# Cross attention of a decoder as one written-out row of 32 rounds: another order of its pieces, queries' weights handled apart, the output one round later

## The chip, the cores and the metric

One core of one Trainium2 chip runs the whole program in one launch. The metric is the device time of that core in microseconds (us), the median of several runs. TensorE (PE) multiplies, VectorE (DVE), ScalarE (ACT) and GpSimd (POOL) work on what it leaves, and SyncE (SP) issues the transfers.

## What is computed

Two decoder layers on x of 4 x 512 x 512, six steps with a layer normalisation after each. The change is in the fifth step alone, the cross attention of layer 1:

```python
q = (hidden_states @ Wq).reshape(B, Sq, H, D)            # B 4, Sq 512, H 16, D 128
k = (encoder_hidden_states @ Wk).reshape(B, Skv, H, D)   # Skv 512, inner size 256
v = (encoder_hidden_states @ Wv).reshape(B, Skv, H, D)
q = rmsnorm(q, gq)
k = rmsnorm(k, gk)
scores = jnp.einsum('bqhd,bkhd->bhqk', q, k) * scale
attn = jax.nn.softmax(scores, axis=-1)
out = jnp.einsum('bhqk,bkhd->bqhd', attn, v)
return out.reshape(B, Sq, H * D) @ Wo
# afterwards: x = _layernorm(x + this)
```

## The kernel before

The function `cross_attention` is one of five stages, each a block with its own instruction stream for each engine. It works in 32 rounds: 4 sequences times 8 pairs of heads. A round has two halves that belong to different pairs. The half called x projects pair n+1 (queries, keys and values, means of squares, transposes); the half called y takes pair n through scores, exponentials, values, sums, quotients and the output projection. `body(b, x, y)` writes both for each engine, and `turns` runs it in two nested loops on the chip (`Fori`), with the first and the last half round outside. Between sequences `start` transposes the next x, and `finish` normalises the last one on VectorE.

Every product of two float32 numbers is made of three passes of split numbers (`split3`, lines 198 to 200), except probabilities times values and the sums of probabilities, which are plain float32. The high half of a weight comes from ScalarE (`Copy`), the low half from GpSimd (`lo`). One load, one high half and one low half cover queries', keys' and values' weights together (`load_proj`, L1870, L1793).

Waits go by semaphores. The eight banks of PSUM are shared out in a fixed turn: the class `Banks` makes a matrix product wait until the one before it in the same bank has been read (`wait_empty`). Before the change the banks 0 to 2 serve the projections and transposes (`pa`), 3 to 5 the scores, the sums and the output (`pb`), 6 and 7 the values. The sum of the probabilities of a head lies over all rows of a bank, and VectorE takes its quotient there (L1926, `reciprocal`), which frees the bank.

TensorE's order in a round is: scores of both heads, values of head 0, half of the queries, sum 0, values of head 1, sum 1, the other half of the queries, four tiles of keys and values, one tile of output, transposes of keys and then of queries, three tiles of output. VectorE's order is: quotient 0, quotient 1, mean of the queries' squares, low halves of the output, queries' normalisation, one output tile, low halves of the transposes, mean of the keys' squares, three output tiles.

Of the kernel before, what the change touches and what calls it, by code (L numbers as in the profile page):

```python
# [1633 lines left out]
def cross_attention(c):  # L1634
# [8 lines left out]
    nc, d = c.nc, c.d  # L1643
    HP = 2
    G = 16 // HP
    NW = HP * DX
    with ExitStack() as ctx:
        def sb(nm, shape, dt=F32):
            return ctx.enter_context(nc.sbuf_tensor(f"s5_{nm}", shape, dt))

# [21 lines left out]
        sq = sb("squares", [P, T, NW])  # L1672
# [4 lines left out]
        probsT = sb("probsT", [P, HP, T, S])  # L1677
        psum2 = sb("probs_pair_sums", [P, 2, S])
        psum1 = sb("probs_sum", [P, HP, S])
# [4 lines left out]
        consts = c.sem("s5_gains_loaded")  # L1684
        bound_ready = c.sem("s5_bound_ready")
        rawx_in = Count(c.sem("s5_w_proj_loaded"), 48)
        rawo_in = Count(c.sem("s5_w_out_loaded"), 16)
        wx_hi = Count(c.sem("s5_w_proj_hi_ready"), 1)
        wx_lo = Count(c.sem("s5_w_proj_lo_ready"), 1)
        wo_hi = Count(c.sem("s5_w_out_hi_ready"), 1)  # L1690
        wo_lo = Count(c.sem("s5_w_out_lo_ready"), 1)
        ctx_in = Count(c.sem("s5_ctx_loaded"), 16)
        ctx_hi = Count(c.sem("s5_ctx_hi_ready"), 1)
        ctx_lo = c.s5_ctx_lo
        squared = {"q": Count(c.sem("s5_q_squared"), 1), "k": Count(c.sem("s5_k_squared"), 1)}
        ms_ready = {"q": Count(c.sem("s5_q_mean_sq_ready"), 1), "k": Count(c.sem("s5_k_mean_sq_ready"), 1)}
        rs_ready = {"q": Count(c.sem("s5_q_rstd_ready"), 1), "k": Count(c.sem("s5_k_rstd_ready"), 1)}
        q_normed = Count(c.sem("s5_q_normed"), 1)
        f_hi = {"qT": Count(c.sem("s5_qT_hi_ready"), HP), "kT": Count(c.sem("s5_kT_hi_ready"), HP)}
        p_sum = Count(c.sem("s5_probs_summed"), HP)  # L1700
        inv_ready = Count(c.sem("s5_inv_sums_ready"), HP)
        o_hi = Count(c.sem("s5_out_hi_ready"), HP)


        pa, pb = c.ps.part(), c.ps.part()
        pa_keys = [("q", 0), ("q", 1)] + [("kv", t) for t in range(T)] + [("kT", 0), ("kT", 1), ("qT", 0), ("qT", 1)]
        pa.open([(k, i % 3, 1) for i, k in enumerate(pa_keys)], outer=c.x_uses([0, 1, 2]))
        pb_keys = [("e", h, k) for h in range(HP) for k in range(T)] + [("y", t) for t in range(T)]
        uses = [(k, 3 + i % 3, 1) for i, k in enumerate(pb_keys)]
        pb.open(uses[:8] + [(("o", 0), 6, 1), (("o", 1), 7, 1), (("sum", 0), 3, 1), (("sum", 1), 4, 1)] + uses[8:])  # L1710
        block = ctx.enter_context(nc.Block())

        def flat(ap):
            return ap.rearrange("p a n -> p (a n)")

        def side(buf, turn):

            return flat(buf[:, bass.ds(turn % 2, 1), :])

        def load_proj(sp, g):  # L1720
            sp.dma_start(raw_x[:, OQ:OKV].rearrange("p (k n) -> p k n", k=KD),
                         d["l1x_wq"].rearrange("(k p) n -> p k n", p=P)[:, :, bass.ds(g * NW, NW)]).then_inc(rawx_in.sem, 16)
            kv = raw_x[:, OKV:].rearrange("p (k a n) -> p k a n", k=KC, a=2)
            for a, nm in ((0, "l1x_wk"), (1, "l1x_wv")):
                sp.dma_start(kv[:, :, a, :],
                             d[nm].rearrange("(k p) n -> p k n", p=P)[:, :, bass.ds(g * NW, NW)]).then_inc(rawx_in.sem, 16)

        def load_out(sp, g):
            sp.dma_start(raw_o[:, :].rearrange("p (h n) -> p h n", h=HP),
                         d["l1x_wo"].rearrange("(h p) n -> p h n", p=P)[:, bass.ds(g * HP, HP), :]).then_inc(rawo_in.sem, 16)  # L1730

        def turns(eng, start, body, finish):

            start(0)
            body(0, (0, 0), None)
            with eng.Fori(0, B - 1) as b:
                with eng.Fori(0, G - 1) as g:
                    body(b, (b, b * G + (g + 1)), b * G + g)
                start(b + 1)
                body(b, (b + 1, b * G + G), b * G + (G - 1))  # L1740
                finish(b)
            b = B - 1
            with eng.Fori(0, G - 1) as g:
                body(b, (b, g + (b * G + 1)), g + b * G)
            body(b, None, b * G + (G - 1))
            finish(b)

        @block.sync
        def _(sp):
            sp.dma_start(gains[:, 0, :], d["l1x_gq"].broadcast_to([P, DX])).then_inc(consts, 16)  # L1750
# [3 lines left out]
            load_proj(sp, 0)  # L1754
            load_out(sp, 0)

            def next_proj(turn, g):
# [140 lines left out]
        def _(dve):  # L1898
# [8 lines left out]
            def body(b, x, y):  # L1907
# [41 lines left out]
                if x is not None:  # L1949
                    mean_squares(0, "q")  # L1950
# [717 lines left out]
```

## Time and profile before

| | |
|---|---|
| median of 3 runs | 2633.09 us (2633.03 to 2633.87) |
| the profiled execution | 2633.11 us, span 2631.3 us |
| TensorE busy over the span | 2218.0 us (84%) |
| VectorE, ScalarE, GpSimd busy | 1409.2 us (54%), 1211.2 us (46%), 910.4 us (35%) |
| mean granted clock of TensorE | 0.939 of full speed |

The span runs from the first to the last instruction. A share of busy time is a mean over five stages; the cross attention has the stretch from 1193.8 to 2327.9 us.

### The profile page before, as it was taken

To read this page: it belongs to the slowest core of one execution; us is meant where nothing else is said; L and a number is where in the kernel's file an instruction comes from. 1 tells how busy PE (TensorE), PEld (TensorE's weight loads), DVE (VectorE), ACT (ScalarE), POOL (GpSimd) and SP (SyncE) were. 2 spreads that over 40 slices of the span, in tenths; PEclk is the share of its full clock that TensorE was granted. 3 is DMA by queue.
4 is the path that set the end of the run, shared out by engine and by line. 5 is a ranking of instruction groups with operands and counts; after the bars stand their busy time and mean duration, and the time that the engine had idled before them with its cause. 6 is when DMAs were issued, how large, how long until landed. Compare 5 with 4: busy or idle time off the path is not lost. (4 is left out here: it accounts for less than half of the span.)

```text
span 2631.3 us, 35761 instructions
## 1 busy us (share of the span) xinstructions
PE 2218.0 (84%) x12440; PEld 1555.7 (59%) x12440; DVE 1409.2 (54%) x2138; ACT 1211.2 (46%) x2272; POOL 910.4 (35%) x570
## 2 busy tenths in 40 slices
PE   6988989858867878875999999999999999957672
PEld 4564655447756645544777777777777677634241
DVE  4666666545544543542555665556555655543445
ACT  3645455343335643524555545554555555522322
POOL 3524244310013211203555545555555555510101
PEclk9999999979888999987999999999999999978795
DMA  3000000010010000003111111121111111020001
GB/s 107 2 1 1 0 2 1 1 60 1 1 44 4 1 1 1 1 1 114 48 48 43 53 48 48 48 72 48 48 48 48 48 48 48 32 95 1 0 0 64
DMA packets 62365, 84.12 MB, mean 32 GB/s; under 512 B 6132, under 2 KB 41332, under 8 KB 61752
## 3 DMA queue, kind: packets, MB, share of 16 engines
q1 hardware_dynamic: 62264, 82.76, 9.3%
q8 instruction: 65, 1.06, 0.2%
q14 instruction: 36, 0.29, 0.0%
HBM read 74.36 MB, written 4.19 MB: 30 GB/s over the span
## 5 line engine op out<-in xcount | busy, mean ns | idle before, releaser
L1926 DVE RECIPROCAL s_inv_sums<-banks 128x512 f32<-128x512 f32 x64 | 214.8, 3356 | 343.3 <-PE banks L2039 340.0
L1800 POOL TENSOR_TENSOR s_qk_rstd<-s_mean_sq,minus_half 128x8 f32<-128x8 f32 x64 | 118.5, 1851 | 502.1 <-DVE s_mean_sq L1913 502.1
L2032 PE MATMUL banks<-s_probsT,s_v 128*128 128x512 f32 x512 | 231.3, 594 | 0.0
L1863 ACT ACTIVATE s_probsT<-banks,s_minus_bound,s_qk_rstd 128x512 f32<-128x512 f32 x256 | 177.0, 781 | 92.6 <-PE banks L200 88.6
L594 DVE TENSOR_REDUCE s_neg_max<-banks 128x1 f32<-128x512 f32 x256 | 165.4, 684 | 88.1 <-PE banks L660 86.5
L543 ACT ACTIVATE s_probsT<-banks 128x512 f32<-128x512 f32 x256 | 148.7, 600 | 81.6 <-PE banks L674 79.2
L198 PE MATMUL banks<-s_w_proj_hi,xT_hi 128*128 (+1 forms) x512 | 170.8, 334 | 2.9 <-DVE s_ctxT_lo L1974 2.9
L1834 ACT ACTIVATE s_squares<-banks 128x512 f32<-128x512 f32 x64 | 38.3, 598 | 286.1 <-PE banks L200 286.0
L2032 PEld LDWEIGHTS banks<-s_probsT,s_v 128*128 128x128 f32 x512 | 97.6, 191 | 111.1 <-issue 108.5
L1793 POOL TENSOR_TENSOR s_w_proj_lo<-s_w_proj_raw,s_w_proj_hi 128x2048 f32 (+1 forms) x33 | 151.9, 4604 | 14.0 <-ACT s_w_proj_hi L1826 14.0
L1809 POOL TENSOR_TENSOR s_probs_pair_sums<-s_probsT 128x1024 f32<-128x1024 f32 x64 | 151.2, 2362 | 7.2 <-issue 7.2
L199 PE MATMUL banks<-s_w_proj_lo,xT_hi 128*128 (+1 forms) x512 | 145.7, 285 | 0.0
L200 PE MATMUL banks<-s_w_proj_hi,xT_lo 128*128 (+1 forms) x512 | 145.7, 285 | 0.0
L482 POOL TENSOR_TENSOR x_cur<-s_probsT 128x512 f32<-128x512 f32 x64 | 82.0, 1281 | 156.8 <-PE banks L692 110.1
L660 PE MATMUL banks<-s_kT,s_qT 128*128 128x512 f32 x256 | 117.8, 464 | 6.9 <-DVE s_neg_max L594 3.3
L198 PE MATMUL banks<-s_wqkv_hi,xT_hi 128*128 128x512 f32 (+1 forms) x256 | 92.1, 360 | 34.6 <-POOL s_wqkv_lo L464 8.8
L674 PE MATMUL banks<-s_qT,s_kT 128*128 128x512 f32 x256 | 106.3, 415 | 16.4 <-ACT s_qT L536 14.2
L198 PEld LDWEIGHTS banks<-s_w_proj_hi,xT_hi 128*128 128x128 f32 x512 | 98.9, 193 | 18.1 <-issue 18.1
L198 PE MATMUL banks<-s_w_out_hi,s_outT_hi 128*128 (+1 forms) x256 | 104.2, 407 | 5.8 <-DVE s_outT_lo L1933 5.8
L199 PEld LDWEIGHTS banks<-s_w_proj_lo,xT_hi 128*128 128x128 f32 x512 | 99.1, 194 | 14.8 <-issue 14.8
L198 PE MATMUL banks<-s_w_proj_hi,s_ctxT_hi 128*128 (+1 forms) x256 | 101.3, 396 | 7.1 <-ACT s_v L1849 7.1
L1959 DVE TENSOR_TENSOR x_all<-banks,x_all 128x512 f32 (+1 forms) x128 | 85.5, 688 | 35.6 <-PE banks L200 32.3
(412 smaller groups left out, 5938.8 us busy)
## 6 DMA issues: line engine op xcount, KB each, us to landing
s_w_proj_raw<-l1x_wq SPq DMA_DIRECT2D x33, 512.0 KB, 4.6
s_w_out_raw<-l1x_wo SPq DMA_DIRECT2D x33, 512.0 KB, 3.6
s_w_proj_raw<-l1x_wk SPq DMA_DIRECT2D x33, 256.0 KB, 4.8
s_w_proj_raw<-l1x_wv SPq DMA_DIRECT2D x33, 256.0 KB, 5.1
x_all<-x SPq DMA_DIRECT2D x4, 1024.0 KB, 12.7
s_ctxT<-ctxT SPq DMA_DIRECT2D x8, 512.0 KB, 5.6
x_cur<-x_all SPq DMA_DIRECT2D x4, 1024.0 KB, 8.2
out<-x_all SPq DMA_DIRECT2D x4, 1024.0 KB, 4.3
```

What stands on the lines that cost most here:

```text
L198: pe.matmul(out, lhs[0], rhs[0], start=start, stop=False)
L199: pe.matmul(out, lhs[0], rhs[1], start=False, stop=False)
L200: return pe.matmul(out, lhs[1], rhs[0], start=False, stop=stop)
L543: act.activation(probsT[:, h % NPB, k, :], ps.ap(s), ACT.Exp).then_inc(ps.freed(s), 1)
L594: dve.tensor_reduce(nmax[:, h % 2, t, 0:1], ps.ap(s), AX.X, ALU.max, negate=True) \
L660: pe.matmul(ps.ap(s), qT[:, h % NQB, t * P:(t + 1) * P], kT[:, h % NKV, :], start=True, stop=True).then_inc(ps.filled(s), 1)
L1793: pool.tensor_tensor(out, raw, hi.bitcast(F32), ALU.subtract).then_inc(done.sem, 1)
L1800: pool.tensor_tensor(rs[:, j, :, :], ms[:, j, :, :], c.mhalf[:, 0:T * HP].rearrange("p (t h) -> p t h", h=HP), ALU.pow) \
L1809: pool.tensor_tensor(psum2[:, :, :], probsT[:, h, 0:2, :], probsT[:, h, 2:4, :], ALU.add)
L1863: act.activation(probsT[:, h, k, :], pb.ap(("e", h, k)), ACT.Exp, bias=bound[:, 0:1], scale=rs[:, 1, k, h:h + 1]).then_inc(pb.freed(("e", ...
L1926: dve.reciprocal(inv[:, h, :], pb.ap(("sum", h))).then_inc(pb.freed(("sum", h)), 1)
L2032: mm = pe.matmul(pb.ap(("o", h)), v[:, k, h * DX:(h + 1) * DX], probsT[:, h, k, :], start=(k == 0), stop=(k == T - 1))
```

## The change

`cross_attention` alone is written anew. There are no loops on the chip any more: a Python list `seq` holds all pieces of all rounds in one row, and each engine's stream is that row with the pieces that concern it. What else differs:

- The order in a round is another, for all engines at once. The output projection of pair j is done in round j+1, its first tile between the two sums. The first sum stands behind the second half of the queries. The two transposes of the queries (`TQ`) stand between the second and the third tile of keys and values, those of the keys (`TK`) near the end.
- On VectorE the mean of the queries' squares (`MQ`) comes first, then quotient 0 (`R`), an output tile, the queries' normalisation (`NQ`), and quotient 1.
- Banks 0 to 2 now serve x transposes, queries, keys and values, transposes and also the sums, in turn. Scores and output share banks 3 to 5.
- Queries' weights have a load, a high half and a low half of their own (`WQ`), keys' and values' weights others (`WK`).
- x is transposed from `x_all` itself, and not from a copy loaded again. `x_cur` holds squares and sums of probabilities instead.
- GpSimd adds the four tiles of probabilities with three additions of 512 columns, before with one of 1024 and one of 512.
- The layer normalisation after a sequence (`L`) is applied by ScalarE, before by VectorE. Its statistics are taken with each output tile.
- At the stage's start the big loads are issued ahead of the four small ones of the gains.

The values were plain float32 before and are so after.

```diff
-    nc, d = c.nc, c.d
...
+    nc, d, ps = c.nc, c.d, c.ps
...
-        sq = sb("squares", [P, T, NW])
+        sq = c.xcur[:, 0:2, :].rearrange("p a (b n) -> p (a b) n", n=NW)
+        psum = c.xcur[:, 2:2 + HP, :]
...
+        seq = [("X", 0, k) for k in range(KD)] + [("WQ", 0), ("Cx", 0), ("WK", 0)]
+        for j in range(-1, N + 1):
+            now, nxt, prv, border = 0 <= j < N, j + 1 < N, 0 <= j - 1, (j + 2) % G == 0 and j + 2 < N
+            if now:
+                seq += [("E", j, 0, k) for k in range(T)] + [("U", j, 0)]
+            if nxt:
+                seq.append(("Q", j + 1, 0))
+            if now:
+                for k in range(T):
+                    seq.append(("E", j, 1, k))
+                    if prv and k < HP:
+                        seq.append(("OH", j - 1, k))
+                seq += [("U", j, 1), ("V", j, 0)]
+            elif prv:
+                seq += [("OH", j - 1, h) for h in range(HP)]
+            if nxt:
+                seq += [("Q", j + 1, 1), ("MQ", j + 1)]
+            if now:
+                seq += [("SU", j, 0), ("R", j, 0)]
+            if border:
+                seq += [("X", (j + 2) // G, k) for k in range(KD)]
+            if j + 2 < N:
+                seq.append(("WQ", j + 2))
+            if prv:
+                seq.append(("O", j - 1, 0))
+            if nxt:
+                seq.append(("NQ", j + 1))
+            if now:
+                seq += [("SU", j, 1), ("V", j, 1), ("R", j, 1)]
+            if nxt:
+                seq += [("KV", j + 1, 0), ("KV", j + 1, 1), ("TQ", j + 1, 0), ("TQ", j + 1, 1),
+                        ("KV", j + 1, 2), ("KV", j + 1, 3), ("MK", j + 1)]
+            if prv:
+                seq += [("O", j - 1, 1), ("O", j - 1, 2)]
+            if nxt:
+                seq += [("TK", j + 1, 0), ("TK", j + 1, 1)]
+            if prv:
+                seq.append(("O", j - 1, 3))
+            if border:
+                seq.append(("Cx", (j + 2) // G))
+            if j + 2 < N:
+                seq.append(("WK", j + 2))
+            if now:
+                seq.append(("WO", j))
+            if prv and j % G == 0:
+                seq.append(("L", j // G - 1))
+
+        uses, na, nb = [], 0, 0
+        for s in seq:
+            if s[0] in ("X", "Q", "KV", "TK", "TQ", "SU"):
...
+            elif s[0] in ("E", "O"):
+                uses.append((s, 3 + nb % 3, 1))
+                nb += 1
+            elif s[0] == "V":
+                uses.append((s, 6 + s[2], 1))
+        ps.open(uses)
...
+            load_q(0)
+            load_ctx(0)
+            load_kv(0)
             sp.dma_start(gains[:, 0, :], d["l1x_gq"].broadcast_to([P, DX])).then_inc(consts, 16)
             sp.dma_start(gains[:, 1, :], d["l1x_gk"].broadcast_to([P, DX])).then_inc(consts, 16)
             sp.dma_start(gcols[:, 0:1], d["l1x_gq_col"]).then_inc(consts, 16)
             sp.dma_start(gcols[:, 1:2], d["l1x_gk_col"]).then_inc(consts, 16)
...
+            load_out(0)
+            for ph, j, *s in seq:
+                if ph == "WQ" and j + 1 < N:
+                    sp.wait_ge(*wq_lo.after(j, 1))
+                    load_q(j + 1)
+                elif ph == "WK" and j + 1 < N:
+                    sp.wait_ge(*wk_lo.after(j, 1))
+                    load_kv(j + 1)
...
+                        .then_inc(wo_lo.sem, 1)
+                elif ph == "MQ":
+                    rstd(0, "q", j)
...
+                elif ph == "U":
+                    h = s[0]
+                    pool.wait_ge(*ps.released(0, ("E", j, h, T - 1)))
...
+                    pool.tensor_tensor(psum[:, h, :], probs[:, h, 0, :], probs[:, h, 1, :], ALU.add)
+                    pool.drain()
+                    pool.tensor_tensor(psum[:, h, :], psum[:, h, :], probs[:, h, 2, :], ALU.add)
+                    pool.drain()
+                    pool.tensor_tensor(psum[:, h, :], psum[:, h, :], probs[:, h, 3, :], ALU.add).then_inc(p_sum.sem, 1)
+                    pool.drain()
...
+            for ph, j, *s in seq:
+                if ph == "X":
+                    k = s[0]
+                    dve.wait_ge(*x_hi.after(j, k + 1))
+                    dve.tensor_tensor(c.xlo[:, k, :], ps.ap(("X", j, k)), c.xhi[:, k, :].bitcast(F32), ALU.subtract) \
...
+                elif ph == "MQ":
+                    mean_squares(0, "q", j)
...
+                elif ph == "NQ":
...
+                elif ph == "R":
+                    h = s[0]
+                    dve.wait_ge(*ps.full(0, ("SU", j, h)))
+                    if j > 0:
+                        dve.wait_ge(*o_lo.after(j - 1, h + 1))
+                    dve.reciprocal(inv[:, h, :], ps.ap(("SU", j, h))).then_inc(ps.freed(("SU", j, h)), 1)
+                    dve.wait_ge(*ps.released(0, ("SU", j, h)))
+                    dve.wait_ge(*ps.full(0, ("V", j, h)))
+                    dve.tensor_tensor(inv[:, h, :], ps.ap(("V", j, h)), inv[:, h, :], ALU.mult) \
+                       .then_inc(ps.freed(("V", j, h)), 1)
...
+                    if j % G == G - 1:
+                        dve.drain()
+                        dve.bn_stats(c.stats[:, t, :], xt)
```

In the diff `E` is a tile of scores and its exponential, `U` GpSimd's sum of exponentials, `V` the values, `SU` the sum over rows on TensorE, `O` a tile of output, `OH` its split input, `Q` and `KV` projections, `X` the transposes of x.

**VectorE in a round in the middle.** Before, from the first quotient of a round on (`s_inv_sums` holds quotients, `s_mean_sq` means of squares):

```order
L1926 RECIPROCAL s_inv_sums<-banks 128x512
L1927 REGISTER_ALU
L1928 REGISTER_ALU
L1929 TENSOR_TENSOR s_inv_sums<-banks,s_inv_sums 128x512
L1925 REGISTER_ALU
L1926 RECIPROCAL s_inv_sums<-banks 128x512
L1927 REGISTER_ALU
L1928 REGISTER_ALU
L1929 TENSOR_TENSOR s_inv_sums<-banks,s_inv_sums 128x512
L1909 REGISTER_ALU
L1910 TENSOR_REDUCE s_mean_sq<-s_squares 128x8
L1913 TENSOR_SCALAR s_mean_sq<-s_mean_sq 128x8
```

After, from the queries' mean of squares on (`x_cur` are the squares, line 1980 the quotient, 1993 the output tile, 1963 the queries' normalisation, 1970 the low half of the queries' transposes):

```order
L1936 TENSOR_REDUCE s_mean_sq<-x_cur 128x8
L1939 TENSOR_SCALAR s_mean_sq<-s_mean_sq 128x8
L1980 RECIPROCAL s_inv_sums<-banks 128x512
L1983 TENSOR_TENSOR s_inv_sums<-banks,s_inv_sums 128x512
L1993 TENSOR_TENSOR x_all<-banks,x_all 128x512
L1963 TENSOR_TENSOR s_q<-s_q,s_qk_rstd 128x1024
L1980 RECIPROCAL s_inv_sums<-banks 128x512
L1983 TENSOR_TENSOR s_inv_sums<-banks,s_inv_sums 128x512
L1970 SCALAR_TENSOR_TENSOR s_qkT_lo<-banks,s_gain_product_column,s_qkT_hi 128x512 x2
L1936 TENSOR_REDUCE s_mean_sq<-x_cur 128x8
L1939 TENSOR_SCALAR s_mean_sq<-s_mean_sq 128x8
L1993 TENSOR_TENSOR x_all<-banks,x_all 128x512 x2
```

The mean of squares has moved ahead of the first quotient, and an output tile and the normalisation now stand between the two quotients.

**TensorE around the sums.** Before, from the end of the first half of the queries on (line 2039 is the sum, 2032 the values):

```order
L200 MATMUL banks<-s_w_proj_hi,xT_lo 128x256
L189 REGISTER_ALU
L2038 ISA
L2039 MATMUL banks<-s_probs_sum,ones_sb 128x512
L187 REGISTER_ALU
L2032 MATMUL banks<-s_probsT,s_v 128x512
L2031 REGISTER_ALU
L2032 MATMUL banks<-s_probsT,s_v 128x512 x2
L2031 REGISTER_ALU
L2032 MATMUL banks<-s_probsT,s_v 128x512
L2038 REGISTER_ALU
L2039 MATMUL banks<-s_probs_sum,ones_sb 128x512
```

After, from the end of the second half of the queries on (2079 is the sum, 2072 the values, `s_w_out` an output tile, `s_ctxT` the first tile of keys and values):

```order
L200 MATMUL banks<-s_w_proj_hi,xT_lo 128x256
L2079 MATMUL banks<-x_cur,ones_sb 128x512
L198 MATMUL banks<-s_w_out_hi,s_outT_hi 128x512
L199 MATMUL banks<-s_w_out_lo,s_outT_hi 128x512
L200 MATMUL banks<-s_w_out_hi,s_outT_lo 128x512
L198 MATMUL banks<-s_w_out_hi,s_outT_hi 128x512
L199 MATMUL banks<-s_w_out_lo,s_outT_hi 128x512
L200 MATMUL banks<-s_w_out_hi,s_outT_lo 128x512
L2079 MATMUL banks<-x_cur,ones_sb 128x512
L2072 MATMUL banks<-s_probsT,s_v 128x512 x4
L198 MATMUL banks<-s_w_proj_hi,s_ctxT_hi 128x512
L199 MATMUL banks<-s_w_proj_lo,s_ctxT_hi 128x512
```

Six products of an output tile have come between the two sums, the second sum stands ahead of the values of head 1, and keys and values follow at once. Before, half of the queries followed.

**The layer normalisation between two sequences.** Before, VectorE at the end of a sequence:

```order
L1979 BN_STATS ln_stats<-x_all 128x6 x4
L328 BN_AGGR ln_mean_var<-ln_stats 128x2 x4
L330 TENSOR_SCALAR ln_var_eps<-ln_mean_var 128x4
L331 REGISTER_ALU
L334 TENSOR_SCALAR x_all<-x_all,ln_mean_var,ln_rstd 128x512 x4
L1736 REGISTER_ALU
L1736 COMPARE_AND_BRANCH
```

After, ScalarE at the end of the round behind a sequence's last (line 1921 is the normalisation, 1909 the next round's exponentials):

```order
L1898 ACTIVATE s_qkT_hi<-banks 128x512 x2
L1868 ACTIVATE s_w_proj_hi<-s_w_proj_raw 128x1024
L1871 ACTIVATE s_w_out_hi<-s_w_out_raw 128x1024
L1921 ACTIVATE x_all<-x_all,s_ln_minus_mean_rstd,ln_rstd 128x512 x4
L1909 ACTIVATE s_probsT<-banks,s_minus_bound,s_qk_rstd 128x512 x4
L1877 ACTIVATE x_cur<-banks 128x512
L1880 ACTIVATE s_q<-banks 128x512
```

The four normalising instructions now stand on ScalarE, in front of the exponentials of the next round's scores.

## Rows read from the trace of the kernel before

**Rows 1.** Busy time of each engine in the stage's middle; the columns are named

```profile
core 0: us, PE busy (x) PEld busy (x) DVE busy (x) ACT busy (x) POOL busy (x), PEclk, DMA share, GB/s
1221.20:2291.00 1069.80, 1037.62 (x4936) 780.02 (x4935) 629.63 (x652) 559.71 (x1028) 561.58 (x253) 1.00 0.15 48
```

**Rows 2.** Waits of TensorE in that stretch: us in total, times, longest

```profile
PE banks L2015 <- DVE s_qkT_lo L1943: 17.3, 32, 0.5
PE banks L198 <- ACT s_v L1849: 7.1, 3, 2.4
```

**Rows 3.** Timeline of TensorE in one round: start, us, what

```profile
1301.05 0.39 PE L198 MATMUL banks<-s_qkT_hi 128*128 128x512 f32 x1
...
1312.80 1.02 PE L2039 MATMUL banks<-s_probs_sum,ones_sb 128*128 128x512 f32 x2
1313.66 3.60 PE L2032 MATMUL banks<-s_probsT,s_v 128*128 128x512 f32 x8
1317.09 1.02 PE L2039 MATMUL banks<-s_probs_sum,ones_sb 128*128 128x512 f32 x2
...
1320.81 0.39 PE L198 MATMUL banks<-s_w_proj_hi,s_ctxT_hi 128*128 x1
...
1326.40 0.39 PE L198 MATMUL banks<-s_w_out_hi,s_outT_hi 128*128 x1
...
1327.77 1.03 PE L2015 MATMUL banks<-ident_sb,s_k 128*128 128x128 f32 x8
...
1334.17 0.39 PE L200 MATMUL banks<-s_w_out_hi,s_outT_lo 128*128 x1
1334.40 0.39 PE L198 MATMUL banks<-s_qkT_hi 128*128 128x512 f32 x1
```

**Rows 4.** Timeline of ScalarE in that round, at the queries' second half

```profile
1321.01 0.60 ACT L1834 ACTIVATE s_squares<-banks 128x512 f32<-128x512 f32 x1 [3.49 <-PE banks L200]
```

**Rows 5.** Timeline of VectorE in that round

```profile
1313.86 3.36 DVE L1926 RECIPROCAL s_inv_sums<-banks 128x512 f32<-128x512 f32 x1 [11.80 <-PE banks L2039]
1317.34 0.69 DVE L1929 TENSOR_TENSOR s_inv_sums<-banks,s_inv_sums 128x512 f32<-128x512 f32 x1
...
1322.24 1.21 DVE L1910 TENSOR_REDUCE s_mean_sq<-s_squares 128x8 f32<-128x1024 f32 x1
...
1323.65 1.30 DVE L1933 TENSOR_TENSOR s_outT_lo<-s_inv_sums,s_outT_hi 128x512 fp32r<-128x512 f32 x2
1326.04 1.23 DVE L1920 TENSOR_TENSOR s_q<-s_q,s_qk_rstd 128x1024 f32<-128x1024 f32 x1 [1.08 <-POOL s_qk_rstd L1800]
```

**Rows 6.** Timeline of TensorE between the first two sequences

```profile
1531.39 0.50 PE L198 MATMUL banks<-s_w_proj_hi,s_ctxT_hi 128*128 x1 [2.36 <-ACT s_v L1849]
```

**Rows 7.** Busy time and clock in two stretches behind that wait, columns as in rows 1

```profile
1532.50:1533.00 0.50, 0.50 (x3) 0.41 (x2) 0.34 (x1) 0.50 (x2) 0.00 (x0) 0.50 0.00 0
...
1535.00:1536.00 1.00, 1.00 (x5) 0.70 (x4) 0.00 (x0) 0.00 (x0) 0.00 (x0) 0.56 0.00 0
```

**Rows 8.** Timeline of the stage's start

```profile
1199.41 0.16 DVE L1900 TENSOR_TENSOR s_gain_product_column<-s_gain_columns 128x1 f32<-128x1 f32 x1 [8.84 <-DMA s_gain_columns<-l1x_gk_col]
...
1202.41 1.91 ACT L1826 ACTIVATE s_w_proj_hi<-s_w_proj_raw 128x2048 fp32r<-128x2048 f32 x1 [8.88 <-DMA s_w_proj_raw<-l1x_wv]
...
1211.60 1.23 DVE L1974 TENSOR_TENSOR s_ctxT_lo<-s_ctxT,s_ctxT_hi 128x1024 fp32r<-128x1024 f32 x1 [0.25 <-ACT s_ctxT_hi L1893]
```

**Rows 9.** Timeline around layer normalisations: ScalarE before the stage, GpSimd in it

```profile
1190.60 2.93 ACT L1439 ACTIVATE x_all<-x_all,s_ln_minus_mean_rstd,ln_rstd 128x512 f32<-128x512 f32 x4 [34.75 <-DVE s_ln_minus_mean_rstd L1538]
...
1509.41 2.36 POOL L1793 TENSOR_TENSOR s_w_out_lo<-s_w_out_raw,s_w_out_hi 128x1024 fp32r<-128x1024 f32 x1
1511.72 1.01 POOL L339 TENSOR_TENSOR ln_rstd<-ln_var_eps,minus_half 128x4 f32<-128x4 f32 x1
```

**Rows 10.** Waits of TensorE from 2290 us on: us in total, times, longest

```profile
PE banks L198 <- DVE s_outT_lo L1933: 5.8, 1, 5.8
PE banks L2039 <- POOL s_probs_sum L1811: 2.3, 1, 2.3
```

More of the change, by code:

```diff
@@ L1728, in load_out @@
[L1728 to L1746, printed above, removed]
+        nmr = sb("ln_minus_mean_rstd", [P, T])
@@ L1785, in _ @@
-            next_out(B * G - 1, 0)
+            load_out(0)
[6 more added lines that the diff above has]
+                    load_kv(j + 1)
+                elif ph == "WO" and j + 1 < N:
+                    sp.wait_ge(*wo_lo.after(j, 1))
+                    load_out(j + 1)
+                elif ph == "Cx" and j + 1 < B:
+                    sp.wait_ge(*ctx_lo.after(j, 1))
+                    load_ctx(j + 1)
@@ L1984, in _, with turned @@
         @block.tensor
         def _(pe):
-            def body(b, x, y):
-                def wx(off, n):
-                    return tuple(side(a, x[1])[:, off:off + n] for a in (wx_h, wx_l))
-                def queries(i):
-                    if i == 0:
-                        pe.wait_ge(*wx_lo.after(x[1], 1))
-                        pe.wait_ge(*ctx_lo.after(x[0], 1))
-                    pa.wait_empty(pe, x, ("q", i))
+            def turned(key, source):
+                ps.wait_empty(pe, 0, key)
+                for t in range(T):
+                    mm = pe.transpose(ps.ap(key)[:, t * P:(t + 1) * P], source(t), c.ident[:, :])
+                mm.then_inc(ps.filled(key), 1)
@@ new lines, in _ @@
+            for ph, j, *s in seq:
+                key = (ph, j, *s)
+                if ph == "X":
+                    turned(key, lambda t: c.x[:, j * T + t, s[0] * P:(s[0] + 1) * P])
+                elif ph == "Q":
+                    i = s[0]
+                    if i == 0:
+                        pe.wait_ge(*wq_lo.after(j, 1))
+                        if j % G == 0:
+                            for k in range(KD):
+                                pe.wait_ge(*ps.released(0, ("X", j // G, k)))
+                    ps.wait_empty(pe, 0, key)
@@ L2028, in values @@
-                def values(h):
-                    pb.wait_empty(pe, y, ("o", h))
-                    for k in range(T):
-                        pe.wait_ge(*pb.released(y, ("e", h, k)))
-                        mm = pe.matmul(pb.ap(("o", h)), v[:, k, h * DX:(h + 1) * DX], probsT[:, h, k, :],
-                                       start=(k == 0), stop=(k == T - 1))
-                    mm.then_inc(pb.filled(("o", h)), 1)
-                def sums(h):
-                    pb.wait_empty(pe, y, ("sum", h))
-                    pe.wait_ge(*p_sum.after(y, h + 1))
-                    pe.matmul(pb.ap(("sum", h)), c.ones[:, :], psum1[:, h, :], start=True, stop=True) \
-                      .then_inc(pb.filled(("sum", h)), 1)
@@ L2053, in body @@
-                if x is not None:
-                    queries(0)
-                if y is not None:
-                    sums(0)
-                    values(1)
-                    sums(1)
-                if x is not None:
-                    queries(1)
-                    for t in range(T):
-                        keys_values(t)
-                if y is not None:
-                    pe.wait_ge(*wo_lo.after(y, 1))
-                    for h in range(HP):
-                        pe.wait_ge(*pb.released(y, ("o", h)))
-                    project_out(0)
@@ L2069, in body @@
-                if x is not None:
-                    transposed("kT", kk, pa.released(x, ("kv", T - 1)))
-                    transposed("qT", q, q_normed.after(x[1], 1))
-                if y is not None:
-                    for t in range(1, T):
-                        project_out(t)
-            def start(b):
-                c.pe_turn_x(pe, b, (b, b * G), pa)
-            turns(pe, start, body, nothing)
-        pa.close(B * G, B)
-        pb.close(B * G)
-        c.close_common()
+                                        (side(wx_h, j)[:, w], side(wx_l, j)[:, w]), k == 0, k == KD - 1)
```

473 lines of the change are left out of this document (231 added, 242 removed).

## The prediction

> **What bounds the kernel now.** The page says TensorE 84% of the span; that is a mean over five stages, so I looked at the changed stage alone, by stretches. In its middle TensorE is busy 1037.6 of 1069.8 us, VectorE 630, ScalarE 560, GpSimd 562, at the full clock [rows 1]. The stage is bound by TensorE, and the most that a better order can take back there is what TensorE waits: 32 us. The list of waits gives them names. Every round has one of 0.54 us between the transposes of keys and queries (17.3 us in 32), and three waits of 2.36 us lie between sequences (7.1 us) [rows 2]. A round in the timeline lasts 1334.40 - 1301.05 = 33.35 us, of which 33.35 - 0.54 = 32.8 us are TensorE's own work [rows 3].
>
> The change removes none of that work: before and after, a round has the same products in the same number format. So I ask only where TensorE waits in the new order, beginning with the bank that each product needs.
>
> **The new wait.** Banks 0 to 2 are given out in turn, and between sum 1 and the first queries' transpose stand two tiles of keys and values; so that transpose gets the bank of sum 1, in every round. It has to wait until quotient 1 has read it. Both sides start from the same event, the end of the second half of the queries.
>
> TensorE's side: sum 0 0.86 us (1313.66 - 1312.80), an output tile 1.37 (1327.77 - 1326.40), sum 1 0.86, values 3.43 (1317.09 - 1313.66), two tiles of keys and values 2 x 1.40 (5.59 for four, from 1320.81 to 1326.40) [rows 3]. Together 9.3 us.
>
> VectorE's side: ScalarE squares the queries 0.20 us after their products end (1320.81 to 1321.01) and takes 0.60 [rows 4]. Then mean of squares with its scaling 1.41 (1322.24 to 1323.65), quotient 0 and its hand-over 3.48 (1313.86 to 1317.34), its product with the values 0.69, the output tile about as long, the normalisation 1.23, less some 0.2 where they overlap, and quotient 1 3.36 [rows 5]. With the hand-over to TensorE: 0.80 + 1.41 + 3.48 + 0.69 + 0.69 + 1.03 + 3.36 + 0.1 = 11.6 us. The sums' input isn't late: GpSimd's three additions of 512 columns end before TensorE gets to either sum.
>
> So TensorE waits 11.6 - 9.3 = 2.3 us, in each round with its own output tile and no x transposes between: 27 of them, 62 us. In round 0 there is no output tile; TensorE loses 1.37 us of cover and VectorE 0.7 us of work, so 3.0 us. Bounds: 1.9 a round if the removed register instructions save VectorE 0.1 at each of its four hand-overs, 2.6 if nothing overlaps.
>
> **What goes.** The 0.54 us in every round: the transposes no longer follow each other closely enough in a bank, -17 us [rows 2]. At the round's end ScalarE now splits two weights (two copies of 1024 columns) with only one output tile on TensorE to cover them; the fourth scores tile then waits for the first exponential by 0.1 us: +3 us, from 0 to +12.
>
> **Between sequences (three times).** The x transposes stand behind sum 0 and take four banks in turn. The third gets the bank of sum 0, free 0.80 + 1.41 + 3.36 = 5.6 us after the queries' end; TensorE is there at 0.86 + 2 x 0.43 = 1.7: 3.9 us. The fourth needs the first one's low half, which VectorE makes behind quotient and product: 1.1 us more. This takes the place of the 2.3 us in that round (counted in neither).
> Then the normalisation, two rounds later. Statistics, GpSimd's power and ScalarE's four instructions stand ahead of the next round's exponentials. GpSimd has two low halves of 2.36 us before it, so its power (1.01) ends about 6.2 us after the round's last product, ScalarE (2.93) at 9.3, the first exponential at 10.1 [rows 9]. TensorE can go on for 2.1 us (nine products of 0.23) [rows 3]: it waits 8 us; 4 if GpSimd were free, 10 with the statistics late. Against that stand 2.4 us of old waits and about 1.6 of smaller ones and clock: 5 + 8 - 4 = +9, three times +27 us (+12 to +36).
>
> **Start and end.** Before, the queries' products can begin when the context's low half is made, 1211.60 + 1.23 = 1212.8 us [rows 8]. After, x isn't loaded again. But VectorE's first instruction waits for the four gains, which now stand behind 1.5 MB of loads; before, the first MB was ready 3 us after them (1202.41 against 1199.41) [rows 8], so I put them at 1199.4 + 3 to 4.5 = 1203, then some 1 us of constants, four x halves in turn with ScalarE and the weights' low half: 1208. -5 us (0 to -8). At the end, the output of pair 30 now lies between the last sums and quotients; its 5.4 us of products cover the waits of 5.8 and 2.3 us [rows 10]: -8 us (-3 to -10).
>
> **The clock.** One of the old waits of 2.36 us was followed by the lower level: it ended at 1531.39 [rows 6], and from 1532.5 to about 1535.8 us the granted clock was 0.50 [rows 7]; the other two of rows 2 show no such drop. 3.3 us at 1.2 instead of 2.4 GHz cost 1.6 us. A new wait of 2.3 us in 31 rounds is of that length; with a drop after a third to a quarter of them, 9 x 1.6 = +14; I take +12. Bounds 0 and 31 x 1.6 = +50.
>
> The page "TensorE: Matmul & The Clock Gate" of the Trainium skill, in its part on the transpose mode, says that transposes don't count as busy for the clock. Here they follow the wait directly, which would make drops more frequent and put the time nearer the upper bound, 2745. No row before has a long wait with transposes behind it.
>
> Sum: 62 + 3 - 17 + 3 + 27 - 5 - 8 + 12 = +77 us. Against the profiled execution's 2633.11 us, which is the median to 0.02: 2710 us.
>
> **Rivals.**
> - *The clock falls after nearly every wait.* For it: the wait recurs each round, with transposes behind it. Against: two of three old ones did nothing. 2710 + 38 = 2748 us. 15%.
> - *The wait is smaller and the ends between sequences are cheaper* (1.9 x 27 = 51, +12 there, no drop): 51 + 3 - 17 + 3 + 12 - 13 = +39, 2672 us. 15%.
> - *The wait is hidden, and the kernel gets faster.* It is one mechanism: VectorE's side must come down to 9.3 us, so the quotient would have to take under 2.2 us instead of 3.36, or start before the queries' squares. Then x transposes lose their wait as well: -17 + 3 + 3 x (8 - 4) - 13 = -15, 2618 us. Against it: the shape and the bank's layout stay as in rows 5, and VectorE's order is fixed. 6%.
> - *No change.* The same mechanism halfway: with VectorE at 9.3 + 0.6 us the new wait only takes the place of the old 0.54, and start, end and borders cancel. 4%. The loops themselves hide nothing: across the end of one, products stand 0.23 us apart (1334.17, 1334.40), as inside a round [rows 3].
>
> The forecast as it stands has 60%. The range reaches over both neighbours: 2672 to 2748. 0.2% (5 us) is about what this kernel's measurement can tell from no change. Slower 0.90, same 0.04, faster 0.06.
>
> **What would show it.** In the waits of TensorE, the transpose line should wait for the quotient (DVE `s_inv_sums`) some 28 times with 2.3 us each; the x transposes for the same line three times with 4 us; scores for ScalarE's exponential three times with 8 us, behind four `x_all` instructions. A round should last 35.3 us. The granted clock in the middle should fall below 1.00. I am wrong if a round lasts under 33.5 us, if the transposes wait for something else, or if TensorE's products themselves stand further apart than 0.23 us, as instructions that arrive too slowly would show.

## The result and the profile after

The kernel after takes 2733.81 us (2731.08 to 2736.98 in 4 runs), the kernel before 2633.06 us in the same job: a ratio of 1.0384, interval 1.0366 to 1.0401, or +100.7 us. The profiled execution took 2731.08 us, its span is 2729.3 us. All of the loss is in the changed stage: the next one starts its first product 2426.33 - 2328.19 = 98.1 us later, and the span is 98.0 us longer.

The waits of TensorE in the stage, which answer to [rows 2] (us in total, times, longest):

```profile
PE banks L2013 <- DVE s_inv_sums L1980: 70.6, 31, 3.6
PE banks L198 <- ACT s_probsT L1909: 24.2, 6, 7.4
PE banks L2013 <- DVE xT_lo L1946: 7.5, 4, 6.8
...
PE banks L2013 <- DVE s_q L1963: 4.5, 1, 4.5
PE banks L198 <- DVE s_qkT_lo L1973: 3.3, 5, 1.0
```

The transposes (L2013) wait for VectorE's quotient (`s_inv_sums`) 31 times. Three of these are transposes of x, 10.9 us together; the other 28 are the queries', 59.7 us or 2.13 us each. Of the 28, 21 last about 1.98 us. The 17.3 us of rows 2 have become 3.3, and the wait for `s_v` between sequences has all but gone. Three of the six waits of the second line, 7.35, 7.36 and 6.99 us, belong to the layer normalisations; 6.8 us of the third line lie at the stage's start.

One round of VectorE, as [rows 5]:

```profile
1618.92 1.22 DVE L1936 TENSOR_REDUCE s_mean_sq<-x_cur 128x8 f32<-128x1024 f32 x1 [5.18 <-ACT x_cur L1877]
...
1620.32 3.36 DVE L1980 RECIPROCAL s_inv_sums<-banks 128x512 f32<-128x512 f32 x1
1623.71 0.69 DVE L1983 TENSOR_TENSOR s_inv_sums<-banks,s_inv_sums 128x512 f32<-128x512 f32 x1
1624.32 0.68 DVE L1993 TENSOR_TENSOR x_all<-banks,x_all 128x512 f32<-128x512 f32 x1
1624.92 1.21 DVE L1963 TENSOR_TENSOR s_q<-s_q,s_qk_rstd 128x1024 f32<-128x1024 f32 x1
1626.05 3.35 DVE L1980 RECIPROCAL s_inv_sums<-banks 128x512 f32<-128x512 f32 x1
```

It works without a gap from 1618.92 to 1629.40, and what starts it is ScalarE's square of the queries (`x_cur`). TensorE in that round, as [rows 3]:

```profile
1603.21 0.39 PE L198 MATMUL banks<-s_qkT_hi 128*128 128x512 f32 x1
...
1629.54 1.07 PE L2013 MATMUL banks<-ident_sb,s_q 128*128 128x128 f32 x8 [1.98 <-DVE s_inv_sums L1980]
1630.37 0.63 PE L198 MATMUL banks<-s_w_proj_hi,s_ctxT_hi 128*128 128x512 f32 x1
1630.80 0.63 PE L199 MATMUL banks<-s_w_proj_lo,s_ctxT_hi 128*128 128x512 f32 x1
...
1639.80 0.39 PE L198 MATMUL banks<-s_qkT_hi 128*128 128x512 f32 x1
```

The transpose starts 0.14 us after quotient 1 has ended. Behind it products stand 0.43 us apart in place of 0.23. This round lasts 1639.80 - 1603.21 = 36.59 us, before 33.35. The granted clock in the stage's middle, then just behind that wait, and a little later (columns as in [rows 1], the clock is the third number from the end):

```profile
1221.20:2300.00 1078.80, 983.04 (x4509) 728.25 (x4510) 570.63 (x583) 523.35 (x975) 523.09 (x320) 0.96 0.14 43
...
1631.00:1633.00 2.00, 2.00 (x6) 1.52 (x6) 1.34 (x2) 0.48 (x1) 0.00 (x0) 0.50 0.00 0
1634.00:1636.00 2.00, 2.00 (x10) 1.60 (x10) 0.59 (x1) 1.04 (x4) 0.00 (x0) 1.00 0.00 0
```

TensorE falls to its lower level, 1.2 of 2.4 GHz, behind the wait and comes back. Below, such a stretch at the lower level is called a drop. To see how often, take the first sum of each round; the distance of two such rows is a round. One sequence of the kernel after:

```profile
1583.09 1.02 PE L2079 MATMUL banks<-x_cur,ones_sb 128*128 128x512 f32 x2
...
1618.09 1.02 PE L2079 MATMUL banks<-x_cur,ones_sb 128*128 128x512 f32 x2
...
1654.67 1.02 PE L2079 MATMUL banks<-x_cur,ones_sb 128*128 128x512 f32 x2
...
1761.57 1.02 PE L2079 MATMUL banks<-x_cur,ones_sb 128*128 128x512 f32 x2
...
1803.25 1.02 PE L2079 MATMUL banks<-x_cur,ones_sb 128*128 128x512 f32 x2
...
1839.85 1.02 PE L2079 MATMUL banks<-x_cur,ones_sb 128*128 128x512 f32 x2
...
1886.99 1.02 PE L2079 MATMUL banks<-x_cur,ones_sb 128*128 128x512 f32 x2
```

Rounds of 35.00 and 36.58 us, three of 106.90 together (35.36, 36.55 and 34.99), then the three at the border of two sequences: 41.68, 36.60, 47.14. An ordinary round is 35.0 us long without a drop of the clock and 36.6 with one. Eight rounds of the same kinds before the change, one sequence earlier, last from 1346.15 to 1620.87 us (first sums, line L2039): 274.72 us against 303.90. Five ordinary ones are 11.8 us longer (178.48 against 5 x 33.34), the three at the border 17.4 (125.42 against 108.0; this border holds the one old drop of [rows 7], the two later ones take 106.5). Over the whole stage, the granted clock of the profiled execution falls behind 15 of the queries' 28 waits, in the ordinary rounds behind every other one.

### The profile page after: what moved, and what is told of

Its sections match the earlier page's. It is cut to its first block and busy times, and to the rows that moved or that the text cites. A ratio compares the mean times of both kernels' runs of the same rounds, so it can differ in the third digit from the quotient of the medians.

```text
span 2729.3 us, 32725 instructions
## 1 busy us (share of the span) xinstructions
PE 2249.9 (82%) x12406; PEld 1570.8 (58%) x12440; DVE 1412.1 (52%) x2127; ACT 1222.1 (45%) x2318; POOL 909.2 (33%) x663
## 5 line engine op out<-in xcount | busy, mean ns | idle before, releaser
L1936 DVE TENSOR_REDUCE s_mean_sq<-x_cur 128x8 f32<-128x1024 f32 x64 | 78.1, 1220 | 248.1 <-ACT x_cur L1877 178.5
L1988 DVE TENSOR_TENSOR s_outT_lo<-s_inv_sums,s_outT_hi 128x512 fp32r<-128x512 f32 x64 | 66.7, 1072 | 241.6 <-ACT s_outT_hi L1916 241.6
L198 PE MATMUL banks<-s_w_proj_hi,xT_hi 128*128 128x256 f32 x512 | 159.7, 312 | 2.9 <-DVE s_w_proj_lo L1957 2.9
L1888 ACT ACTIVATE x_cur<-banks 128x256 f32<-128x256 f32 x128 | 49.3, 385 | 251.4 <-PE banks L200 251.2
L199 PE MATMUL banks<-s_w_proj_lo,xT_hi 128*128 128x256 f32 x512 | 146.8, 287 | 0.0
L200 PE MATMUL banks<-s_w_proj_hi,xT_lo 128*128 128x256 f32 x512 | 146.7, 286 | 0.0
L198 PE MATMUL banks<-s_qkT_hi 128*128 128x512 f32 x256 | 106.3, 415 | 27.5 <-ACT s_probsT L1909 24.2
L198 PE MATMUL banks<-s_w_proj_hi,s_ctxT_hi 128*128 128x512 f32 x256 | 125.1, 489 | 0.5 <-ACT s_v L1894 0.5
L198 PE MATMUL banks<-s_w_out_hi,s_outT_hi 128*128 128x512 f32 x256 | 115.9, 453 | 1.6 <-DVE s_outT_lo L1988 1.6
L199 PE MATMUL banks<-s_w_proj_lo,s_ctxT_hi 128*128 128x512 f32 x256 | 109.0, 426 | 0.0
```

The costliest lines, as they stand in the source:

```text
L198: pe.matmul(out, lhs[0], rhs[0], start=start, stop=False)
L199: pe.matmul(out, lhs[0], rhs[1], start=False, stop=False)
L200: return pe.matmul(out, lhs[1], rhs[0], start=False, stop=stop)
```

## The experiments

Times are medians with their ranges; the ratio is to the kernel before in the same job. Each is an edit of the kernel after, or of the experiment it names.

**e1: the sums take their turn in banks 3 to 5.**

```diff
-            if s[0] in ("X", "Q", "KV", "TK", "TQ", "SU"):
+            if s[0] in ("X", "Q", "KV", "TK", "TQ"):
...
-            elif s[0] in ("E", "O"):
+            elif s[0] in ("E", "O", "SU"):
```

> The changed kernel with one edit: the two sums of a round take their turn in banks 3 to 5 with scores and output, no longer in banks 0 to 2. Theory A (the queries' transpose waits for the bank of sum 1): the 31 waits of about 2.3 us (70.6 us) vanish, the clock no longer falls behind them, and the time drops from 2734 to about 2635 us (2620 to 2650). Rival B (VectorE's chain as a whole is too late, whatever the bank): the transpose then waits for the queries' normalisation, for 1 us or more a round, and the time stays above 2690. Rival C (the long instruction stream slows TensorE): the waits vanish, but products stand further apart than 0.23 us and the time stays above 2680.

Measured: 2684.08 us (2683.41 to 2685.3), ratio 1.0192 (1.0175 to 1.0209). That is 49.7 us less than the kernel after, where theory A asked for about twice as much. Rival C also has a time above 2680 us, but not its cause: at full clock two products of 512 columns start 0.23 us apart in the median, as in both kernels. Its waits:

```profile
PE banks L198 <- ACT s_probsT L1909: 24.2, 6, 7.4
PE banks L2013 <- DVE xT_lo L1946: 20.8, 4, 6.9
PE banks L198 <- DVE s_qkT_lo L1970: 20.2, 28, 1.4
```

The wait for the quotient has gone entirely, so the bank of the sum was its cause. But two others came up behind it, 20.2 us in the rounds and 13.3 more at the x transposes. The row of one:

```profile
1616.86 0.50 PE L198 MATMUL banks<-s_w_proj_hi,s_ctxT_hi 128*128 128x512 f32 x1 [0.57 <-DVE s_qkT_lo L1970]
```

The fourth tile of keys and values takes the bank of the first queries' transpose. Its low half is made on VectorE, and there it still stands behind quotient 1. I had followed the bank of the sum and not VectorE's queue.

**e2: eight more products ahead of the queries' transposes**, with a result that is not used, in the time of the wait.

```diff
+                        pe.wait_ge(*ps.released(0, ("KV", j, 0)))
+                        for _ in range(8):
+                            pe.matmul(ps.ap(("TQ", j, 1)), c.xhi[:, 0, 0:P], side(wx_h, j)[:, 0:512], start=True, stop=True)
```

> The changed kernel with eight extra products of 512 columns (1.8 us) in front of the queries' transposes, into the bank that the second transpose overwrites; their result is used by nobody. Theory A (the waits cost twice: 70 us directly, and some 35 us by the lower clock behind them): VectorE sets the moment of the transposes, so the extra work is free, the granted clock in the stage's middle is 1.00 nearly everywhere, and the time is about 2700 us (2690 to 2710). Rival B (the clock costs next to nothing, and the rest of the loss lies elsewhere): 2734 us or slower. Rival C (TensorE, not VectorE, sets the moment of the transposes): 31 x 1.8 = 56 us more, 2790 us.

Measured: 2714.16 us (2712.79 to 2716.83), ratio 1.0308 (1.0291 to 1.0325), 19.6 us less than the kernel after for 8 products more in a round, and 4 us above theory A's range. Rounds at the first sums:

```profile
1613.67 1.02 PE L2082 MATMUL banks<-x_cur,ones_sb 128*128 128x512 f32 x2
...
1648.65 1.02 PE L2082 MATMUL banks<-x_cur,ones_sb 128*128 128x512 f32 x2
...
1684.00 1.02 PE L2082 MATMUL banks<-x_cur,ones_sb 128*128 128x512 f32 x2
```

34.98 and 35.35 us: rounds without a drop. The median of its rounds is 35.0 us, and outside the borders none is over 35.4. From 1221.20 to 1400.00 us its granted clock is 1.00, where the kernel after has 0.97. None of the 15 drops behind the queries' transposes is left. The 19.6 us are less than they cost, because the three rounds with the x transposes have no such wait to hide the extra products in: from first sum to first sum these rounds take 44.40, 44.55 and 44.51 us, where the kernel after has 41.85, 41.68 and 43.23, together 6.7 us more. From the stage's first scores to its last, all other rounds together are 24 us shorter, which is 15 times 1.6 us. The six drops behind the waits of the x transposes and of the normalisations stay.

**e3: the layer normalisation after the next round's exponentials.**

```diff
+                if j > G and j % G == 1:
+                    seq.append(("L", j // G - 1))
...
-            if prv and j % G == 0:
-                seq.append(("L", j // G - 1))
+            if j == N:
+                seq.append(("L", B - 1))
```

> The changed kernel with one edit: the layer normalisation between sequences is applied behind the next round's exponentials instead of ahead of them. Theory A (TensorE waits 7.4 us three times for exponentials that stand behind ScalarE's four normalising instructions): 22 us of waits and some 5 us of lower clock go, about 2707 us (2700 to 2714). Rival B (the wait comes from elsewhere in that round, such as the late bank of an output tile): at most 5 us less, above 2725 us.

Measured: 2709.87 us (2708.67 to 2713.45), ratio 1.0293 (1.0276 to 1.031), -23.9 us.

```profile
PE banks L2015 <- DVE s_inv_sums L1982: 70.6, 31, 3.6
...
PE banks L198 <- ACT s_probsT L1911: 2.5, 3, 0.8
```

The wait for the exponentials falls from 24.2 to 2.5 us, and the quotient's stays to the tenth. The two waits are independent, and what leaves the list leaves the time. The drops are not as steady: behind the queries' transposes this profile has 19 of them, the kernel after 15.

**e4: e1 and e3 together, the x transposes in pairs around the output tiles, and the four small loads first.**

```diff
-            if border:
-                seq += [("X", (j + 2) // G, k) for k in range(KD)]
...
+            if border:
+                seq += [("X", (j + 2) // G, k) for k in (0, 1)]
             if prv:
                 seq += [("O", j - 1, 1), ("O", j - 1, 2)]
+            if border:
+                seq += [("X", (j + 2) // G, k) for k in (2, 3)]
```

> Sums in banks 3 to 5, the normalisation behind the next round's exponentials, the x transposes in the second half of the round, two by two around output tiles, and the small loads first at the stage's start. Theory A: a round takes TensorE's own 32.8 to 32.9 us, with no wait left between sequences: 31 x 0.45 = 14 us less than before the change in the rounds, some 12 between sequences, 8 at the start and 8 at the end: 2633 - 42, about 2592 us (2580 to 2610), faster than both kernels. Rival B (another wait of 0.5 us a round takes the old one's place, the fourth scores tile behind two weight copies): 2600 to 2625 us.

Measured: 2640.26 us (2638.98 to 2641.83), ratio 1.0026 (1.0016 to 1.0036). Of the excess 93.6 us are gone, but 48 us of theory A's are missing, and rival B's 2600 to 2625 us are passed as well. The wait of e1 recurs in every round, and so does a small one for ScalarE's copy of the values:

```profile
PE banks L198 <- DVE s_qkT_lo L1974: 21.9, 31, 1.4
...
PE banks L198 <- ACT s_v L1898: 4.2, 28, 0.2
```

**e5: e4 with the queries' transposes behind all four tiles of keys and values.**

```diff
-                seq += [("KV", j + 1, 0), ("KV", j + 1, 1), ("TQ", j + 1, 0), ("TQ", j + 1, 1),
-                        ("KV", j + 1, 2), ("KV", j + 1, 3), ("MK", j + 1)]
+                seq += [("KV", j + 1, 0), ("KV", j + 1, 1), ("KV", j + 1, 2), ("KV", j + 1, 3),
+                        ("TQ", j + 1, 0), ("TQ", j + 1, 1), ("MK", j + 1)]
```

> The version with all repairs (sums in banks 3 to 5, normalisation later, x transposes later, small loads first), and the queries' transposes behind the fourth tile of keys and values instead of behind the second. Theory A: the 0.57 us that the fourth tile waited in each round for the low half of the first queries' transpose (which VectorE makes behind quotient 1) go, and a round takes 33.0 us instead of 34.1: 2640 - 31 x 1.0 = about 2609 us (2600 to 2618), faster than the kernel before. Rival B (the wait moves on to the keys' transposes, whose bank then waits for the same low half): 2630 us or more.

Measured: 2619.95 us (2619.04 to 2621.18), ratio 0.9945 (0.9928 to 0.9962): 0.5% faster than the kernel before, and 2 us above theory A's range. An ordinary round takes 33.3 us, where theory A had 33.0. The wait of the keys and values for quotient or low half has gone. One is left at the next round's first scores:

```profile
PE banks L198 <- DVE s_qkT_lo L1977: 18.1, 29, 2.3
```

**e6: that same edit in the kernel after alone.** The third tile of keys and values now takes the bank of sum 1, with products behind the wait in place of transposes.

> The changed kernel with one edit: the queries' transposes behind the fourth tile of keys and values, so that the third tile now gets the bank of sum 1. Theory A (the bank makes the wait, not the transposes' input): the third tile waits for quotient 1, again 2.3 us in 27 rounds and about 70 us in all, on the line of the products. If it is the wait alone that makes the clock fall, the time stays at 2734 us (2728 to 2740). Theory A2 (transposes behind a wait count as further idleness for the clock): same waits, but the clock falls after few of them, and the time is 2710 to 2718 us. Rival B (the transposes waited for the normalisation of the queries as well): the waits shrink by 1 us or more a round, below 2700 us.

Measured: 2748.01 us (2746.8 to 2749.92), ratio 1.0428 (1.0411 to 1.0445).

```profile
PE banks L198 <- DVE s_inv_sums L1980: 57.2, 28, 2.7
PE banks L198 <- DVE s_qkT_lo L1973: 17.8, 30, 2.2
...
PE banks L2013 <- DVE s_inv_sums L1980: 10.9, 3, 3.6
```

The wait for the quotient moves from the transposes to whatever takes the bank of sum 1, with nearly its whole size (68.1 of 70.6 us): it goes by the bank and not by the operation. The time is 8 us above theory A's range all the same. The second line, the scores' wait for the low half of the keys' transposes, had 3.3 us in the kernel after and has 17.8 here, but other waits are shorter (the exponentials' 24.2 us are 15.9), and much of the 14 us by which this run is slower is a lower clock. So theory A2 fell, which wanted fewer drops without transposes behind the wait:

```profile
1221.20:2300.00 1078.80, 979.24 (x4411) 719.24 (x4410) 555.30 (x575) 510.14 (x959) 512.47 (x312) 0.95 0.13 43
```

0.95 with products behind the wait, 0.96 with transposes; 19 of the 28 waits are followed by a drop, 15 of 28 with transposes. The comparison isn't clean, as the new wait lies in the same rounds.

**e7: quotient 1 over 256 of its 512 columns**, used for both halves. It leaves out the quotients of the other 256 columns.

```diff
+                    if h == 0:
+                        dve.reciprocal(inv[:, h, :], ps.ap(("SU", j, h))).then_inc(ps.freed(("SU", j, h)), 1)
+                    else:
+                        dve.reciprocal(half[:, :], ps.ap(("SU", j, h))[:, 0:S // 2]).then_inc(ps.freed(("SU", j, h)), 1)
```

> The changed kernel with quotient 1 taken of 256 columns instead of 512, and used for both halves (the quotient of the other half is left out). Theory A (each microsecond of VectorE's chain before the bank is free is a microsecond of wait): quotient 1 takes 1.7 us instead of 3.36, the wait falls from 2.3 to 0.6 us in 28 rounds, 48 us, and the drops of the clock go with it, 20 to 30 us: about 2660 us (2650 to 2672). Rival B (only the drops' cause lies there, or another wait of over 1 us stands right behind): 2690 us or more.

Measured: 2667.00 us (2666.79 to 2669.34), ratio 1.0125 (1.0108 to 1.0142), -66.8 us.

```profile
1607.65 1.75 DVE L1984 RECIPROCAL s_half_quotient<-banks 128x256 f32<-128x256 f32 x1
...
PE banks L2023 <- DVE s_half_quotient L1984: 14.9, 28, 1.2
PE banks L2023 <- DVE s_inv_sums L1982: 10.9, 3, 3.6
```

The quotient is 1.6 us shorter, and each of the 28 waits it ends is shorter by 1.6 us ((70.6 - 10.9) / 28 = 2.13, now 0.53). 44.8 us of waits have gone. The other 22 us are mostly the clock: from 1600 to 2100 us it is 0.99 where the kernel after has 0.96, and none of the 28 shorter waits, 0.4 to 1.2 us each, is followed by a drop.

**e8: e5 with the keys' transposes ahead of the third output tile.**

```diff
-                seq += [("O", j - 1, 1), ("O", j - 1, 2)]
+                seq.append(("O", j - 1, 1))
...
-                seq.append(("O", j - 1, 3))
+                seq += [("O", j - 1, 2), ("O", j - 1, 3)]
```

> The kernel e5_transposes_last (2619.95 us) with one edit: the two transposes of the keys stand ahead of the third tile of output in place of behind it. What is left in a round of e5 is a wait of 0.34 to 0.6 us in which the next round's first scores wait for the low half of the keys' transposes (18.1 us in 29). Theory A (only that order is at fault): the low half is made one output tile earlier, 1.37 us of products at full clock, more than the wait; the transposes of the keys still have an output tile between them and the low half of the queries' transposes, so no other bank wait comes up. The 18.1 us go, most of the time: 2619.95 - 18 = 2602 us (2600 to 2607), and the list of TensorE's waits has no line of the stage over 5.5 us. Theory B (each such wait has a successor, as after e1 and e4): taking it away uncovers another in the same round, which would be the keys' transposes waiting for the low half of the queries' transposes, since VectorE has the mean of the keys' squares between them: 0.3 to 0.5 us a round, 2610 to 2618 us.

Measured: 2612.94 us (2611.28 to 2613.73), ratio 0.9921 (0.9907 to 0.9934), the fastest of all. The time is in theory B's range, 6 us above theory A's:

```profile
PE banks L198 <- DVE x_all L1997: 7.1, 30, 0.4
...
PE banks L198 <- DVE s_qkT_lo L1977: 5.8, 5, 2.0
```

The wait of e5 is gone from the ordinary rounds, and a successor of 0.24 us has come, another one than theory B named: the scores' bank waits until VectorE has added the output tile that was in it.

## Why the prediction was right, and what was off

The mechanism held, at the place and for the reason forecast. The size didn't quite: +100.7 us where the sum had +77, and the miss is almost all in one term, the clock.

**The direction and the main wait.** "So TensorE waits 11.6 - 9.3 = 2.3 us": 2.13 us in the mean of 28, 1.98 in most rounds, at the operation and for the instruction named, ended by a row of VectorE without a gap. e1 shows that the bank is the cause, e6 that it is the bank's next user that waits, e7 that the quotient's length sets the size. The steps on VectorE hold to two tenths: 1618.92 to 1629.40 is 10.5 us, forecast 1.41 + 3.48 + 0.69 + 0.69 + 1.03 + 3.36 = 10.7. From the start of sum 0 at 1618.09, where the queries' products have ended, TensorE reached the transpose after 9.47 us (forecast 9.3) and the bank was ready for it after 11.45 (forecast 11.6).

**The ordinary round.** Forecast 2.3 - 0.54 = +1.76 us without the clock; measured 35.0 - 33.34 = +1.66. Two small errors cancel: the wait is 1.98 us, and the rest of the round is 33.0 us where the forecast kept 32.8.

**Between sequences.** The x transposes: forecast 3.9 and 1.1 us, these rows (timeline of TensorE, behind the sum at 1761.57):

```profile
1767.21 1.12 PE L2013 MATMUL banks<-ident_sb,x_all 128*128 128x128 f32 x4 [3.65 <-DVE s_inv_sums L1980]
1768.53 1.11 PE L2013 MATMUL banks<-ident_sb,x_all 128*128 128x128 f32 x4 [0.20 <-DVE xT_lo L1946]
...
1872.55 0.80 PE L198 MATMUL banks<-s_qkT_hi 128*128 128x512 f32 x1 [7.36 <-ACT s_probsT L1909]
```

The second of the two, 0.9 us too high, was a step of the forecast that did not hold. The normalisation was forecast at 8 us and waits 7.36; e3 took 21.7 us off that line of the waits, and 23.9 off the time.

**Start and end.** The queries' products begin at 1206.44 us where I had 1208 (before: 1212.8), but 4.5 us of that are given back at the first transposes, for a reason that I did not see (below). The two waits of [rows 10], 8.1 us, are 1.6 and 1.7.

**The clock: the term that was mis-sized.** "With a drop after a third to a quarter of them [...] I take +12." The price of one drop was right: 36.58 - 35.00 = 1.6 us. Their number was not. Behind the queries' transposes there are 15 in 28 waits, where I had 9 in 31, and e2 shows their cost, 24 us. Each border has two more, behind waits that the forecast put no clock to: at the x transposes (first row) and behind the normalisation (third; the second is the transposes' wait of the round between, columns as in [rows 1]):

```profile
1768.00:1770.00 2.00, 1.79 (x8) 1.37 (x7) 1.69 (x3) 0.91 (x2) 0.00 (x0) 0.50 0.00 0
1853.50:1855.50 2.00, 2.00 (x7) 1.62 (x6) 1.50 (x2) 0.80 (x2) 0.00 (x0) 0.50 0.00 0
1873.00:1875.00 2.00, 2.00 (x8) 1.71 (x8) 0.00 (x0) 1.59 (x3) 0.00 (x0) 0.50 0.00 0
```

Some of these six last longer. One of each kind in full:

```profile
2070.90:2077.65 6.75, 6.21 (x16) 4.28 (x17) 4.85 (x8) 2.14 (x3) 2.32 (x1) 0.50 0.00 0
1565.70:1572.50 6.80, 3.92 (x15) 3.63 (x16) 0.00 (x0) 4.94 (x8) 1.27 (x1) 0.50 0.13 48
```

In the six, TensorE is busy for 23.5 us at the lower level; half of that, about 12 us, is an estimate of what they cost, and no run takes those six away alone. Together that is about 36 us, less 2 for the old drop: 34, where the sum had 12.

The terms against each other, as an estimate from the two timelines (measured, then forecast): the queries' wait +60 and +65; the rest of the rounds -10 and -14; the borders without the clock +26 and +27; the start -2 and -5; the end -9 and -8; the clock +34 and +12. The stretches are those from first scores to first scores; the output projection that moved from the first round to the end is counted in neither, and the end includes two old drops. The measured ones add up to 99 us, and the two profiled spans differ by 98.0. So no large term is left without a name, and the measured time, 24 us above the forecast, lies closer to the first rival's 2748 than to the 2710 that had 60%.

The sentence of the Trainium skill on transposes ("TensorE: Matmul & The Clock Gate", "Part 4: PE-mode transpose") would have put the time near 2745. The measured time is 11 us below that, and the drops came for another reason: in e6 products stand behind the wait, and the clock is no better, 0.95 against 0.96. That transposes make the drops more frequent isn't borne out here. What decides whether a wait of 2.0 to 2.8 us is followed by a drop stays open: 15 of 28 were, the four of 2.7 to 2.8 us among them, and none of e7's 28 waits of 0.4 to 1.2 us.

**The rivals.** "The clock falls after nearly every wait" had 2748 and was half true: 15 of the queries' 28 waits and all six of the long ones at the borders. "Hidden" and "no change" fell with the first row of the waits. The forecast that the fourth scores tile would wait behind ScalarE's two weight copies by 0.1 us in each round was wrong: the ordinary rounds show no such wait.

**What I got wrong in the experiments.** Theory A missed by 49 us at e1 and 48 at e4, and by 11 to 14 us at e2, e5, e6 and e8. At e1, e4, e5 and e8 it was one error: a wait that is taken away is replaced by the next later thing on the same path. In e1 that was a low half which waits in VectorE's queue behind the same quotient. e5 removed it by order alone.

## What to carry to other kernels

A result that is read slowly must not lie in a bank whose next user is near in the order: write down for each bank who reads it last and what that reader has queued before, and compare both sides from their common event. Then do it again for each instruction behind the slow one on its engine, since those are the next wait once the first has gone. Short waits in a stage bound by TensorE are to be priced with the clock: here a recurring wait of 2.1 us cost 1.6 us more in about every second round.

## What the hardware showed that I had not expected

**VectorE and GpSimd hold each other up.** At the stage's start, the queries' normalisation beside GpSimd's low half of a weight:

```profile
1218.12 2.34 POOL L1822 TENSOR_TENSOR s_w_proj_lo<-s_w_proj_raw,s_w_proj_hi 128x1024 fp32r<-128x1024 f32 x1
1218.19 3.35 DVE L1963 TENSOR_TENSOR s_q<-s_q,s_qk_rstd 128x1024 f32<-128x1024 f32 x1 [1.75 <-POOL s_qk_rstd L1816]
```

It takes 3.35 us in place of 1.23 [rows 5], and ends 1.08 us after GpSimd's has ended at 1220.46: as if it had done next to nothing before. This is 2.1 of the 4.5 us that the first transposes wait. The output's low half in the round shows it as well, `1611.49 2.25` for its two instructions in place of 1.30 [rows 5], and over the stage 1072 ns in the mean (page of the kernel after, L1988). The Trainium skill says so ("SBUF — State Buffer", "Who interferes with whom"): a VectorE instruction with two inputs in SBUF and a GpSimd instruction that reads SBUF exclude each other, and whichever starts first holds the ports. Both of these have two such inputs, and the trace agrees. The products of quotients and values, with one input in PSUM, keep their 0.69 us beside the same work of GpSimd: the one at 1623.71 lies within a weight's low half (`1622.08 2.35 POOL L1822`).

**A quotient costs five times another operation of its size**: 3.36 us for 128 x 512 (64 in the stage), 1.75 for 128 x 256, and 0.69 for a product of 128 x 512 from the same memory. The Trainium skill names an iterated division in the pipe, with a repeat count of 8 ("VectorE: DVE Perf Modes", "First, the fixed hardware budget"). That count is not the ratio of the times, which is 3.36 / 0.69 = 4.9 here.
